# Causal bias by blocks of 64 keys with triangles in quarters of TensorE's array, and cross keys masked by the mask's row alone

## The reference, cut to what matters

```python
# self attention: 16 heads of 16, causal
scores = jnp.einsum('bqhd,bkhd->bhqk', q, k) * SCALE
causal_bias = (1.0 - jnp.tril(jnp.ones((t, t), dtype=x.dtype))) * -10000.0
attn = jax.nn.softmax(scores + causal_bias, axis=-1)
out = jnp.einsum('bhqk,bkhd->bqhd', attn, v)
...
# cross attention: 16 heads of 16, 512 queries, 1601 keys
Q = (query @ Wq.T + bq)...; K = (key @ Wk.T + bk)...; V = (value @ Wv.T + bv)...
Q = apply_rope(Q, cos_q, sin_q)
K = apply_rope(K, cos_k, sin_k)
scores = jnp.einsum('bhqd,bhkd->bhqk', Q, K) * SCALE
neg_inf = jnp.finfo(scores.dtype).min
scores = jnp.where(mask[:, None, None, :] == 0, neg_inf, scores)
attn = jax.nn.softmax(scores, axis=-1)
```

## Time and profile before

| what | value |
|---|---|
| runs | 1838.22, 1852.01, 1853.08 us (median 1852.01) |
| profiled execution | 1846.2 us, its span 1844.4 us |
| busy, share of the span | PE 91%, DVE 75%, ACT 57%, POOL 37% |
| mean granted TensorE clock | 0.955 |
| self heads | about 780 to 1016 us |
| output projection of the self attention, then keys, queries and values | 1016 to 1148 us |
| cross heads | from 1148 us |

### The profile page before, as it was taken

How to read it: one execution, slowest core, us unless ns; L and a number is a source line. 1 busy time by engine, 2 the same in 40 slices (tenths; PEclk the granted TensorE clock), 3 DMA queues, 4 the chain that set the end, 5 groups by cost and what they waited for, 6 DMA issues and landing times. The chain is left out here.

```text
span 1844.4 us, 34342 instructions
## 1 busy us (share of the span) xinstructions
PE 1686.9 (91%) x13310; PEld 916.1 (50%) x13310; DVE 1376.5 (75%) x2360; ACT 1052.5 (57%) x1764; POOL 686.6 (37%) x770
## 2 busy tenths in 40 slices
PE   8998999899999998889999887699999999999996
PEld 4886777668888885423332654122222222223564
DVE  4535888756676666778784788998999999994774
ACT  4322555345665563446666333177888888887552
POOL 2783777034544443413330343214412121111453
PEclk9999999999999999969999998599999999999998
DMA  6163999687876773601110586321201011000001
GB/s 219 54 214 137 308 322 326 221 308 290 312 294 265 293 296 129 178 11 35 28 36 2 179 227 191 63 64 43 82 20 37 19 28 29 19 20 1 24 12 35
DMA packets 114006, 247.62 MB, mean 134 GB/s; under 512 B 28154, under 2 KB 82974, under 8 KB 110240
## 3 DMA queue, kind: packets, MB, share of 16 engines
q1 hardware_dynamic: 87028, 207.68, 32.3%
q0 software_dynamic: 24176, 35.12, 7.3%
q10 hardware_dynamic: 2640, 2.62, 0.4%
HBM read 183.39 MB, written 61.38 MB: 133 GB/s over the span
## 5 line engine op out<-in xcount | busy, mean ns | idle before, releaser
L2198 DVE TENSOR_REDUCE Eh_maxima<-Eh_max 128x2 f32<-128x802 f32 x512 | 474.8, 987 | 25.1 <-PE Eh_max L2077 20.6
L2186 ACT ACTIVATE Eh_probs<-Eh_pair 128x1024 f32<-128x1024 f32 (+1 forms) x288 | 287.7, 999 | 112.7 <-PE Eh_pair L2116 112.7
L2077 PE MATMUL Eh_max<-Eh_KS,Eh_QS 49*128 49x401 f16 x1024 | 200.1, 360 | 44.8 <-DVE Eh_maxima L2198 40.9
L2139 PE MATMUL Eh_av_ps<-Eh_probs,E_V 128*17 128x512 f32 (+1 forms) x1664 | 225.5, 615 | 0.0
L1537 PE MATMUL C_y<-C_x_high,C_W 128*128 128x256 f16 (+1 forms) x1536 | 214.8, 253 | 9.5 <-ACT C_gate L1597 7.4
L2198 DVE TENSOR_REDUCE Dh_maxima<-Dh_max 128x2 f32<-128x1024 f32 x128 | 152.1, 1221 | 45.0 <-PE Dh_max L2085 43.0
L1537 PE MATMUL C_y<-C_x_low,C_W 128*128 128x256 f16 (+1 forms) x768 | 180.5, 252 | 0.0
L2186 ACT ACTIVATE Eh_probs<-Eh_single 128x512 f32<-128x512 f32 x272 | 161.5, 594 | 31.7 <-PE Eh_single L2116 31.6
L1915 POOL DMA_DIRECT2D Eh_KS<-E_kd x64 | 37.1, 580 | 355.3 <-PE Eh_pair L2116 350.1
L2077 PEld LDWEIGHTS Eh_max<-Eh_KS,Eh_QS 49*128 49x128 f16 x1024 | 50.9, 94 | 235.3 <-DVE Eh_maxima L2198 199.7
L1537 PEld LDWEIGHTS C_y<-C_x_high,C_W 128*128 128x128 f16 x1536 | 139.0, 98 | 22.9 <-ACT C_gate L1597 9.6
(11 more groups left out here) (457 smaller groups left out, 3527.0 us busy)
## 6 DMA issues: line engine op xcount, KB each, us to landing
C_W<-w_split SPq DMA_DIRECT2D x24, 3072.0 KB, 11.4
w_split<-B_w_parts SPq DMA_DIRECT2D x24, 768.0 KB, 9.8
Eh_KS<-E_kd POOLq DMA_DIRECT2D x64, 150.1 KB, 3.3
C_tail<-in_expert_tail_dram SPq DMA_DIRECT2D x24, 384.0 KB, 8.3
B_places<-in_w_experts_dram SPq DMA_DIRECT2D x10, 768.0 KB, 8.3
early_more<-in_w_experts_dram SPq DMA_DIRECT2D x8, 768.0 KB, 11.0
early_ctxT<-in_ctxT_dram SPq DMA_DIRECT2D x6, 800.5 KB, 5.9
early_ctxT<-in_w_experts_dram SPq DMA_DIRECT2D x6, 768.0 KB
```

What stands on the lines that cost most here:

```text
L2077: last = self.nc.tensor.matmul(bank[:, a, 0:self.cw], self.QS[r, slot, p, qt * P:(qt + 1) * P], self.KS[r, slot, p, k0:k0 + self.cw], star ...
L2139: last = self.nc.tensor.matmul(self.av_ps[u * STRIP:u * STRIP + VW, :], self.V[0:r, kt, unit * VW:(unit + 1) * VW], self.probs[0:r, self.b ...
L2186: self.nc.scalar.activation(dst, src, ACT.Exp, scale=1.0 / SCORE).then_inc(self.exp_done, 1)
L2198: self.nc.vector.tensor_reduce(self.maxima[:, g % 2, :, p * TPB + qt, c], self.max_ps[n % 2][:, :, 0:self.cw], AX_X, ALU.max).then_inc(sel ...
```

## The change: what it does

1. **Self heads.** The constant rows carry the bias between blocks of 64 keys: seven rows instead of three (`CAUSAL = S // HALF - 1`, `block = np.arange(S) // HALF`). What is left are two triangles of 64x64 on the diagonal of each block of 128. `triangles` adds them with two matmuls of 64 rows, 64 columns and 64 moving columns, in two quarters of the array that have the rows of the unit's own half.
2. **Cross keys.** `keep`, the multiplication with it and `row` are gone. The mask is loaded once as 4 rows of 1601. VectorE makes the row of penalties of all batches at once (`mask_terms`, ahead of item 2), and SP stores it in one transfer ahead of the store of item 1. The factor 64 moves from `keep` into the table `rotary`; the queries are scaled back.
3. **A batch with no key kept.** VectorE works out one flag for each batch; TensorE spreads the four flags over the partitions with one small matmul ahead of the first query item; VectorE copies them and multiplies each query item with its batch's flag.
4. `MASK` is 16360 instead of 32768.

```diff
-MASK = 32768.0
+MASK = 16360.0
...
     def bias_maxima(self, pe, n, m):
         qt = self.max_parts(m)[3]
         for a in range(2):
-            last = self.nc.tensor.matmul(self.max_ps[n % 2][:, a, qt * P:(qt + 1) * P], self.ident_score[:], self.tri[:, 0, :], start=False, stop=True,
-                                         skip_group_check=True)
+            last = self.triangles(self.max_ps[n % 2][:, a, qt * P:(qt + 1) * P], a, 0)
         last.then_inc(self.filled, 1)
+
+    def triangles(self, block, a, side):
+
+        rows = slice(a * HALF, (a + 1) * HALF)
+        for d in range(2):
+            own = slice(d * HALF, (d + 1) * HALF)
+            last = self.nc.tensor.matmul(block[own, own], self.ident_score[rows, rows], self.tri[rows, side, rows], start=False, stop=True,
+                                         tile_position=(a * HALF, d * HALF), skip_group_check=True)
+        return last
...
-            kt = i // STRIPS
-            last = self.nc.tensor.matmul(self.score_bank(i)[:, kt * P:(kt + 1) * P], self.ident_score[:], self.tri[:, 1, :], start=False, stop=True,
-                                         skip_group_check=True)
+            kt, u = divmod(i, STRIPS)
+            last = self.triangles(self.score_bank(i)[:, kt * P:(kt + 1) * P], u % 2, 1)
...
-CAUSAL = TPB - 1
+CAUSAL = S // HALF - 1
...
-            def load_mask(n):
-                b, _, c0, w = part_of(key_at[n])
-                if n >= RING:
-                    sp.wait_ge(keep_ready, n - RING + 1)
-                sp.dma_start(mask[:, c0:c0 + w], dram["mask"][b, :, c0:c0 + w]).then_inc(mask_loaded[n % RING], 16)
...
-                load_mask(c)
+                if c == 0:
+                    sp.dma_start(mask[:], dram["mask"]).then_inc(mask_loaded, 16)
...
-                if n is not None:
-                    sp.wait_ge(row_ready, n + 1)
-                    sp.dma_start(mask_rows[b, :, :, c0:c0 + w], mask_row[:, n % 2:n % 2 + 1, 0:w].broadcast_to([1, 2, w])).then_inc(row_stored[n % 2], 16)
+                if p == 1:
+                    sp.wait_ge(row_ready, 1)
+                    sp.dma_start(mask_rows[:, 0], mask_row[:].rearrange("b (a w) -> b a w", a=1).broadcast_to([B, 2, S2])).then_inc(row_stored, 16)
...
                 if b == 0:
                     pe.wait_ge(w_scaled, 3)
+                    pe.wait_ge(each_ready, 1)
+                    pe.wait_ge(row_ones, 1)
+                    pe.wait_ge(after.copied_back, KD * B)
+                    mm(after.turn_ps[0][:, 0:B], ones[:], each[:], start=True, stop=True).then_inc(any_product, 1)
...
-                    row(n)
-                    if n >= 2:
-                        values(n)
+                if n is not None and n >= 2:
+                    values(n)
                 high(p)
...
-                v.tensor_scalar(keep[:, n % 2, 0:w], mask[:, c0:c0 + w], 0.0, SCALE, ALU.not_equal, ALU.mult).then_inc(keep_ready, 1)
+            def mask_terms():
+
+                dve.wait_ge(mask_loaded, 16)
+                v.tensor_scalar(mask_row[:], mask[:], 0.0, -MASK, ALU.is_equal, ALU.mult).then_inc(row_ready, 1)
+                dve.wait_ge(row_ready, 1)
+                v.tensor_reduce(masked[:, 0:1], mask_row[:], AX_X, ALU.max).then_inc(count_ready, 1)
+                dve.wait_ge(count_ready, 1)
+                v.tensor_scalar(masked[:, 1:2], masked[:, 0:1], 0.0, None, ALU.is_equal).then_inc(flag_ready, 1)
+                dve.wait_ge(flag_ready, 1)
+                v.tensor_scalar(each[:], ident[0:B, 0:B], masked[:, 1:2], None, ALU.mult).then_inc(each_ready, 1)
...
                 if kn is None:
+                    if b == 0:
+                        dve.wait_ge(any_product, 1)
+                        v.tensor_copy(any_kept[:], after.turn_ps[0][:, 0:B]).then_inc(any_ready, 1)
+                        dve.wait_ge(any_ready, 1)
+                    v.tensor_scalar(t[:, n % 2, :, 0:w], t[:, n % 2, :, 0:w], any_kept[:, b:b + 1], None, ALU.mult).then_inc(kept, 1)
+                else:
                     dve.sem_inc(kept, 1)
-                else:
-                    v.tensor_tensor(t[:, n % 2, :, 0:w], t[:, n % 2, :, 0:w], keep[:, kn % 2:kn % 2 + 1, 0:w].broadcast_to([P, 2, w]),
-                                    ALU.mult).then_inc(kept, 1)
...
-        "mask": np.repeat(a["mask_BxS2_if1"][:, None, :], P, axis=1),
+        "mask": a["mask_BxS2_if1"],
```

More of the change, by code:

```diff
@@ L2836, in phase_cross1 @@
     key_at = [p for p, (_, c) in enumerate(items) if c is not None]
-    row_stored, *stored = ([ctx.enter_context(nc.semaphore(f"E_{n}{i}")) for i in range(2)] for n in ("row_stored", "stored0_", "stored1_"))
+    row_stored = ctx.enter_context(nc.semaphore("E_row_stored"))
+    stored = [[ctx.enter_context(nc.semaphore(f"E_{n}{i}")) for i in range(2)] for n in ("stored0_", "stored1_")]
     places = HeadPlaces(ctx, nc, "Eh", S2, 1, False, qd, kd, mask_rows, (dram["cross_k_rows"], dram["cross_q_rows"]), loaded, 1,
-                        [(row_stored[i], 16 * (KEYS // 2)) for i in range(2)] + [(stored[i][m], 16 * (ITEMS // 2)) for i in range(2) for m in range(2)])
+                        [(row_stored, 16)] + [(stored[i][m], 16 * (ITEMS // 2)) for i in range(2) for m in range(2)])
     tiles = [list(range(3 * c, 3 * c + 3)) for c in range(KC)]
@@ L2852, in phase_cross1 @@
         rotary = sb("rotary", [P, 4, S2])
-        mask = sb("mask", [P, S2], I32)
-        keep = sb("keep", [P, 2, CW], BF16)
+        mask = sb("mask", [B, S2], I32)
+        mask_row, masked, any_kept = sb("mask_row", [B, S2], F16), sb("masked", [B, 2]), sb("any_kept", [P, B])
+        each, ones = sb("each", [B, B]), sb("ones", [B, P])
         halves = sb("halves", [P, 2 * KD * S2], F16)
-        mask_row = sb("mask_row", [1, 2, CW], F16)
         t, other = sb("t", [P, 2, 2, S]), sb("other", [P, 2, S])
@@ L2865, in phase_cross1 @@
         w_scaled, w_high, w_low, bias_scaled = (sem(n) for n in ("w_scaled", "w_high", "w_low", "bias_scaled"))
-        ctx_loaded, mask_loaded = sems("ctx_loaded", RING), sems("mask_loaded", RING)
+        ctx_loaded, mask_loaded = sems("ctx_loaded", RING), sem("mask_loaded")
         bias_loaded = sem("bias_loaded")
         product, rotated, summed, kept, high_ready, low_ready = (sem(n) for n in ("product", "rotated", "summed", "kept", "high_ready", "low_ready"))
-        keep_ready, row_ready = sem("keep_ready"), sem("row_ready")
+        row_ready, count_ready, flag_ready, each_ready, row_ones = (sem(n) for n in ("row_ready", "count_ready", "flag_ready", "each_ready", "row_ones"))
+        any_product, any_ready = sem("any_product"), sem("any_ready")
         v_product, v_copied, chunk_read = sem("v_product"), sem("v_copied"), sem("chunk_read")
@@ L2997, in values @@
                     o.then_inc(v_copied, 1)
-            def row(n):
-                w = part_of(key_at[n])[3]
-                if n >= 2:
-                    act.wait_ge(row_stored[n % 2], 16 * (n // 2))
-                act.wait_ge(keep_ready, n + 1)
-                nc.scalar.activation(mask_row[:, n % 2, 0:w], keep[0:1, n % 2, 0:w], ACT.Copy, bias=-MASK, scale=MASK / SCALE).then_inc(row_ready, 1)
             def high(n):
@@ L3034, in first_gpsimd @@
             nc.gpsimd.memset(V[:].rearrange("p k (u v) -> p (k u) v", v=VW)[:, :, DH:VW], 1.0).then_inc(ones_ready, 1)
+            nc.gpsimd.memset(ones[:], 1.0).then_inc(row_ones, 1)
             for i, (signal, scale) in enumerate(((wk_loaded, E_WEIGHT), (wv_loaded, E_WEIGHT))):
@@ L3052, in first_loads @@
             def first_loads(a):
+                pool.wait_ge(row_stored, 16)
                 for i in range(2):
-                    pool.wait_ge(row_stored[i], 16 * (KC // 2))
                     for m in range(2):
@@ L3081, in first_vector @@
                 bias = bq if kn is None else bk
+                if n == 2:
+                    mask_terms()
                 if kn is not None:
-                    keep_of(kn)
                     if kn < KC:
@@ L3416, in lay_out @@
     causal_tri = np.where(np.stack([i > j, j > i], axis=1), -10000.0, 0.0).astype(np.float16)
-    block = np.arange(S) // P
+    block = np.arange(S) // HALF
     stacks = lambda rows, n, slots: np.repeat(np.array(rows, np.float16).reshape(-1, 1, n), 2 * slots, axis=1)
```

13 lines of the change are left out of this document (3 added, 10 removed).

## The result

The changed kernel takes 1820.8 us in the median of 4 runs (1813.73 to 1825.45), the kernel before beside it 1846.24 (1838.22 to 1853.08): ratio 0.9883, 95% interval 0.9855 to 0.9911. By the ratio that is 21.6 us less, by the interval 16 to 27; the two medians lie 25.4 apart. Forecast were 23 less, and 1829 from a median before of 1852.01. The profiled execution took 1820.29 us, span 1818.4, mean granted clock 0.959 (before 1846.2, 1844.4, 0.955).

The account below looks back on a forecast made before the run. TensorE was taken to bound the self heads, VectorE through ScalarE the key and query items, with TensorE close behind. 1846.2 - 12 - 11 = 1823 for the profiled execution, 1852.0 - 23 = 1829 us on the median; range 1810 to 1848.

Parts of the forecast that it names:

- Part 1: Self heads: triangles added in quarters that run side by side, shape changes still paid; 12 us less.
- the forecast's 12.5: Self heads: expected period of one group in us, instead of 13.24.
- The 0.26: Self heads: expected TensorE time in us of a four-unit bias block, instead of 0.33.
- the load: Self heads: weight load of each quarter, taken at 0.027 us, the same as the stream of a piece.
- rival D: Self heads: quarters don't pay, weight loads stand open; 0.042 us a piece costs 12 us, 0.102 gives 1911; 6%.
- estimate of 53 ns a load in series: Self heads: 64-column weight loads without Fast Weight Load, all in series, cost 1.5 us more a period, 22 in all.
- Rival B: Self heads: the shape changes go too, period about 11 us, VectorE bounds; 1811 us in all; 12%.
- Part 2: Key and query items: without `keep` and mask rows, 11 us less, between 4 and 15.
- each of the four waits loses 1.5 "and more": Key items: TensorE's waits for ScalarE's copies before the last 6 value matmuls shrink; 7 of 10.6 us taken.
- the prediction's sign: Key and query items: TensorE's waits for ScalarE's copies at 3 to 4 us instead of 10.6.
- the row was worth 0.57: Key items: ScalarE's mask row ahead of the copy of values goes, 0.57 us off the chain.
- Half of 3.8: Query items: two queries at part of the clock ran 3.8 us too long; shorter TensorE idle returns 2.

Follow-up runs that it names:

- part1: The kernel before with only the triangles in quarters, `keep` and mask rows unchanged: ratio 0.9903 to the kernel before.
- pieces_twice: The changed kernel with every quarter matmul of the triangles issued twice: ratio 0.9946 to the kernel before.
- same_shape: The changed kernel with each triangle quarter's matmul in its neighbours' shape, 64 rows by 128 columns, zeros beside the identity: ratio 0.9813 to the kernel before.
- act_order: The changed kernel, but ScalarE copies the values of item p + 1 before it casts item p: ratio 0.9837 to the kernel before.
- low_short: The changed kernel with GpSimd's low-part subtraction covering 8 columns of each item from the third on: ratio 0.9872 to the kernel before.
- dve_more: The changed kernel with one more VectorE operation in each key item, where the multiplication with `keep` stood: ratio 0.9925 to the kernel before.
- after_again: The changed kernel, unchanged, profiled once more in one execution: 1827.71 us.
- before_again: The kernel before, unchanged, profiled once more in one execution: 1838.46 us.

## Why the prediction was right, and where its steps were not

**Part 1.** The mechanism is as put: the quarters run side by side, and the change of shape stays. `part1` gives 12.39 for the period, the forecast's 12.5 less 0.1. The sizes: two units were forecast at 0.15 and took 0.15 to 0.16, four at 0.26 and took 0.19. The 0.26 does not follow from the prediction's own terms, 0.11 for the quarters and 0.10 for the changes of shape, which give 0.21. Of the 0.19, 0.09 is the quarters', where 0.11 was taken: a first round of them costs about 0.05 and a second 0.04. The term that was too large is the load, taken at 0.027 for each quarter beside its stream; `pieces_twice` shows load and stream together at 8 to 9 ns. Counted over the 13 blocks, 2 x 0.14 + 4 x 0.09 + 5 x 0.06 + 2 x 0.01 = 0.96 us less, of which 0.85 reached the period (forecast 0.8 and 0.7). The self heads took 13.9 less in the first pair, 9 to 14 over all pairs of traces, and 12.7 with the clock at half for as long in both; forecast 12. The spread is the cold start's.

The Trainium skill, TensorEngine Tiling (Array Packing), Key Properties, says that a change of tiling mode drains TensorE and gives no price; `same_shape` agrees: 0.10 us on each side between 64x128 and 64x64, none without a change. For rival D the Trainium skill, TensorEngine Tiling (Array Packing), Restrictions, says that column tiling disables Fast Weight Load; whether it was off here no run shows. The prediction's estimate of 53 ns a load in series is refuted, since 8 more quarters with their loads cost 0.07 us.

**Rival B** had it right in kind that without shape changes TensorE no longer sets the period alone. It was priced at about 11, from 9.8 of TensorE's work and 10.5 of VectorE's; measured 11.88, with TensorE busy 133.37 / 145 x 11.88 = 10.9 of it and VectorE 10.4. The rest is waiting of the two and ScalarE for each other; which buffer holds it was not tested.

**Part 2** was forecast at 11 and gave 8.7 in the first pair of traces, of which the clock's share is that of the two slow queries, 1.62 + 2.18 = 3.8. Without slow queries the stage went from 95.4 to 90.5 (96.4 and 90.9 in the second traces): 4.9, where 9 were forecast with 2 for the clock beside. The step that was too large is that each of the four waits loses 1.5 "and more", taken as 7 of 10.6: TensorE's waits for ScalarE's copies fell by 3.5, to 7.1, where the prediction's sign was 3 to 4. Two things stood behind. ScalarE casts an item before it copies the values of the next, and a cast may wait for a store (14.8 us of such waits after the change, 11.1 before): `act_order` returns 4.3. And the additions now fall beside GpSimd's subtractions more often, 5.8 us lost instead of 3.9: `low_short` returns 4.2, part of it time that before lost too and part of it perhaps the earlier stores'. That the multiplication was the chain is shown by `dve_more`; that the row was worth 0.57 in each wait isn't: 13 rows cost 1.1 at most.

The small terms: `mask_terms` took 0.99 + 1.81 + 0.14 + 0.79 = 3.7 us (forecast 3.4), covered as put; a query's multiplication 0.75 (taken 1.0, bounds 0.66 to 1.23); the copy of flags 0.16 (0.3); the context's transfer had TensorE wait 1.1 (forecast 2.0 and 1 more).

**The clock.** Half of 3.8 was taken. Before lost 3.8 in one trace and 1.7 in the other, after nothing and 3.3. `after_again` has both slow queries with the same 1.87 us of idle time ahead that the first trace of after has, and in `before_again` the query behind 2.60 us of idle time ran at the full clock. So the premise of the step, that shorter idle time of TensorE ahead of a query gives the clock back, did not decide it; what does stays open. Such stretches cost 1.4 us in the cross heads, 1.5 to 2.3 in a query and some 5 in the longest cold start, and they fall in one execution and not the next. They are enough for most of the 15 us between the runs of one kernel; that they are all of it was not shown.

That the total came out 1.4 us from the forecast by the ratio is partly luck: part 1 gave 1 to 2 more than its 12, part 2 without the clock 4 less than its 9, and the clock, forecast at 2, gave 3.8 in the first pair of traces and between 1.6 lost and 3.8 gained over all pairs. Of the 26.0 us between the profiled executions 4.2 are the cross heads', which the change does not touch.

## What to carry to other kernels

Small matmuls on TensorE between large ones have a price at their borders beside their own. Try the neighbours' tile shape for them, even with zeros in the weights: here smaller pieces took 0.85 us off the period, and the neighbours' shape 0.51 more, until other engines held it. An operation taken off VectorE is worth what the next link of the chain lets through, so look what the consumer's queue does ahead of its wait (here a cast that waits for a store) and what GpSimd runs beside the operations that are left. Before a difference of one stage is explained, trace both kernels twice, and compare how long the clock was at half in it.

## What the runs showed of the hardware

- Quarter matmuls of 64x64, fp16, 64 columns each: 8 to 9 ns for one more, with its weight load (`pieces_twice`: 0.07 us for 8). Weights of the shape 64x128 beside 64x512 matmuls of the same shape: the next starts when the stream of the last is over (0.22 us for two), with 0.09 to 0.10 added at each change to 64x64 (`same_shape` and after).
- A VectorE addition of two fp32 operands nearly stops beside a GpSimd subtraction that began first: 0.96 us alone, 2.03 with 1.21 of overlap. Where the addition began first, it kept its time (1.10) and the subtraction took 2.43 instead of 1.65. The `scalar_tensor_tensor` that reads PSUM kept its time beside the same subtraction (0.61 at 1069.28).
- TensorE's granted clock fell to 1.2 GHz for about 3.4 us in stretches of the cross heads in which it was over 90% busy (31.67 of 34.00), in one execution and not in the next of the same program. At the start of the self heads it stayed there for 34.1 to 47.8 us in the traces of before, after and each part, and for 34.1 and 44.4 in two executions of after.
